# The context of keys and values in a linear-attention kernel: which operand stands, and who adds up the exponentials

## The reference

```python
qp = _softmax_kernel(q, proj[l], True)      # exp(scores - norm - row max) + 1e-4
kp = _softmax_kernel(k, proj[l], False)     # exp(scores - norm - max over all nodes) + 1e-4
k_sum = kp.sum(axis=2)
d_inv = 1.0 / einsum('bhnm,bhm->bhn', qp, k_sum)
ctx = einsum('bhnm,bhnd->bhmd', kp, v)
attn = einsum('bhnm,bhmd,bhn->bhnd', qp, ctx, d_inv)
```

## Time and profile before

| | |
|---|---|
| median of 3 runs | 1161.78 us (1157.0 to 1170.48) |
| profiled execution | 1162.99 us, span 1161.2 us |
| TensorE busy | 1088.6 us (94%) |
| VectorE, ScalarE, GpSimd busy | 697.2 (60%), 363.6 (31%), 148.2 us (13%) |
| context matmuls (line 706) | 512 records, 65.3 us |
| `at` matmuls (line 717) | 512 records, 61.6 us |
| attention stage of layer 0, layer 1 | about 119 to 230, 545 to 661 us of the span |

### The profile page before, as it was taken

One profiled execution on the slowest core, in us unless ns is written; L12 is line 12 of the kernel. 1 busy time (PEld: TensorE's weight loads), 2 busy tenths in 40 slices (PEclk: granted clock), 3 DMA queues, 4 the chain that ended last, 5 costly groups with the idle time before them and its releaser, 6 DMA issues.

```text
span 1161.2 us, 16045 instructions
## 1 busy us (share of the span) xinstructions
PE 1088.6 (94%) x5960; PEld 877.3 (76%) x5960; DVE 697.2 (60%) x1524; ACT 363.6 (31%) x667; POOL 148.2 (13%) x141
## 2 busy tenths in 40 slices
PE   3989799999999999998899999999999999999976
PEld 3767789888777777776898977777777888777632
DVE  7565677479676567457565479674753117723556
ACT  4234466525321311235466415221300012002222
POOL 4230202000000001200102000000000705000026
PEclk8998999999999999989899999999999999999999
DMA  6220101003311112000101003211247201100001
GB/s 211 97 100 1 38 2 38 1 5 91 91 47 63 56 46 78 0 1 1 38 1 38 1 5 115 71 61 50 96 156 252 73 1 37 35 1 1 1 18 55
DMA packets 34653, 60.15 MB, mean 52 GB/s; under 512 B 19440, under 2 KB 20400, under 8 KB 33936
## 3 DMA queue, kind: packets, MB, share of 16 engines
q1 hardware_dynamic: 12688, 41.21, 10.5%
q10 hardware_dynamic: 21888, 17.87, 4.8%
HBM read 48.59 MB, written 10.49 MB: 51 GB/s over the span
## 4 chain that ended last, share of the span: by engine, by line
PE 79%; DVE 10%; ACT 5%; issue 4%; POOL 1%; DMA 0%; ACTq 0%; POOLq 0%; DVEq 0%
PE ps_a L515 10%; PE ps_a L516 10%; PE ps_a L517 10%; PE ps_v L515 9%; PE ps_v L517 8%; PE ps_v L516 8%; PE ps_a L866 5%; PE ps_v L706 5%; PE ps_v L829 2%; PE ps_v L717 2%; PE ps_a L536 2%; PE ps_a L641 2%; DVE expk L1502 2%; ACT work L1037 2%; ACT expk L998 1%
## 5 line engine op out<-in xcount | busy, mean ns | idle before, releaser
L515 PE MATMUL ps_a<-ht_hi,w_hi 128*128 128x512 f32 x488 | 194.6, 399 | 2.7 <-DVE w_lo L1768 0.9
L516 PE MATMUL ps_a<-ht_lo,w_hi 128*128 128x512 f32 x488 | 191.9, 393 | 0.0
L517 PE MATMUL ps_a<-ht_hi,w_lo 128*128 128x512 f32 x488 | 191.6, 393 | 0.0
L948 ACT ACTIVATE work<-ps_a,col_sb 128x512 f32<-128x512 f32 x96 | 66.6, 719 | 203.0 <-PE ps_a L517 144.8
L515 PEld LDWEIGHTS ps_a<-ht_hi,w_hi 128*128 128x128 f32 x488 | 92.7, 190 | 26.1 <-DVE headmask_r L1467 1.3
L517 PEld LDWEIGHTS ps_a<-ht_hi,w_lo 128*128 128x128 f32 x488 | 92.7, 190 | 20.1
L516 PEld LDWEIGHTS ps_a<-ht_lo,w_hi 128*128 128x128 f32 x488 | 92.8, 190 | 19.3
L1621 DVE TENSOR_TENSOR xm<-ps_v,xm 128x512 f32<-128x512 f32 x80 | 55.2, 690 | 86.1 <-PE ps_v L517 85.7
L515 PE MATMUL ps_v<-w_hi,f_hi 128*128 128x512 f32 x256 | 101.7, 397 | 0.0
L517 PE MATMUL ps_v<-w_hi,f_lo 128*128 128x512 f32 x256 | 99.7, 389 | 0.0
L516 PE MATMUL ps_v<-w_lo,f_hi 128*128 128x512 f32 x256 | 99.6, 389 | 0.0
(11 more groups left out here) (228 smaller groups left out, 1941.3 us busy)
## 6 DMA issues: line engine op xcount, KB each, us to landing
stage<-wstream SPq DMA_DIRECT2D x62, 512.0 KB, 3.6
adj_d<-adj_win ACTq DMA_DIRECT2D x16, 256.0 KB, 2.9
adj<-adj_d ACTq DMA_DIRECT2D x2, 2048.0 KB, 12.1
xt_d<-xt_hi SPq DMA_DIRECT2D x2, 1024.0 KB, 5.0
xt_d<-xt_lo SPq DMA_DIRECT2D x1, 2048.0 KB, 11.4
ht_hi<-xt_d ACTq DMA_DIRECT2D x1, 2048.0 KB, 7.9
ht_lo<-xt_d ACTq DMA_DIRECT2D x1, 2048.0 KB, 12.8
x_again<-x ACTq DMA_DIRECT2D x8, 256.0 KB, 9.0
```

The source lines that it names most:

```text
L515: nc.tensor.matmul(ps, left[0], right[0], start=first, stop=False)
L516: nc.tensor.matmul(ps, left[0], right[1], start=False, stop=False)
L517: return nc.tensor.matmul(ps, left[1], right[0], start=False, stop=last)
L948: nc.scalar.activation(work[:, n % 4, :], psA[:, i % BANKS, :], func, **how).then_inc(a_empty, 1)
```

## The change

The operands of the context change places. The values of one head (64 columns) are now the stationary operand, and the exponentials of its node tile stream, all 256 features at once. The two heads of a pair stand on the left and right 64 columns of the array and write the upper and lower 64 partitions of one bank. The result is the context turned round, so VectorE copies it to `ctx_t`, and a new job, `turn_ctx`, turns it back with two transposes; VectorE copies that to `ctx_sb`. The columns of ones are gone from the products. In their place GpSimd adds up the 8 exponential tiles of each head with three adds (`k_part`, `k_sum`), and `turn_ctx` sums `k_sum` over the partitions by four matmuls with one column of ones. `ctx` moves to the end of step 1; `turn_ctx` stands where `ctx` stood. On GpSimd weight 3's split moves from pair 0 to pair 1, behind the adds.

```diff
@@ attention_order, ring_v_attention
         if s == 2 and g < STEPS:
-            yield "ctx", pair
+            yield "turn_ctx", pair
         if 1 <= g <= STEPS:
             yield "tr", g - 1
         if g >= 2:
             yield "at", g - 2
+        if s == 1 and g < STEPS:
+            yield "ctx", pair
...
-        elif what in ("ctx", "at"):
+        elif what in ("ctx", "turn_ctx"):
+            yield what, g
+        elif what == "at":
             yield from ((what, g, j) for j in range(2))
@@ tiles
-        ctx_sb = at("ctx_sb", [P, 2, 2, MT, DH + 1], f32, "ctx")
+        ctx_sb = at("ctx_sb", [P, 2, MT, 2, DH + 1], f32, "ctx")
+        ctx_t = at("ctx_t", [P, M], f32, "ht", 16 * KB)
+        k_part = at("k_part", [P, NT // 2, M], f32, "ht", 18 * KB)
+        k_sum = at("k_sum", [P, 2, M], f32, "ht", 22 * KB)
@@ TensorE
+                    elif what == "ctx":
+                        ps = bank("v", ("ctx", g))
+                        pe.wait_ge(expk_done, L * NH * NT + (2 * g + 2) * NT)
+                        if g == 0:
+                            pe.wait_ge(vsum_added, L * (NT - 1) + NT)
+                        for t in range(NT):
+                            for j in range(2):
+                                head = slice(DH * j, DH * (j + 1))
+                                nc.tensor.matmul(ps[head, 0:M], V[:, t, g, 1 + DH * j:1 + DH * (j + 1)],
+                                                 expk[g % 2][:, j, t, :], start=t == 0, stop=False)
+                        nc.tensor.matmul(ps[:, 0:M], vsum[:, g, 1:1 + P], eps_k[:].to_broadcast([P, M]), start=False,
+                                         stop=True).then_inc(v_full, 1)
+                    elif what == "turn_ctx":
+                        ps = bank("v", ("turn_ctx", g))
+                        written_v(("ctx", g))
+                        for m in range(MT):
+                            nc.tensor.transpose(ps[:, nodes(m)], ctx_t[:, nodes(m)], ident[:])
+                        pe.wait_ge(k_summed, L * NH + 2 * g + 2)
+                        for m in range(MT):
+                            for j in range(2):
+                                last = nc.tensor.matmul(ps[:, M + 2 * m + j:M + 2 * m + j + 1], k_sum[:, j, nodes(m)],
+                                                        V[:, 0, 0, 0:1], start=True, stop=True)
+                        last.then_inc(v_full, 1)
...
-                                    written_v(("ctx", pair, j))
+                                written_v(("turn_ctx", pair))
@@ GpSimd
                     nc.gpsimd.partition_all_reduce(kall[:, pair, :], kmax1[:, pair, :], P, RMAX).then_inc(kall_ready, 1)
                     if pair == 0:
+                        pool.wait_ge(a_full, a0 + (MIX_A[QK_ORDER[-1]] + 1))
+                    for j in range(2):
+                        done_ = 2 * (L * NH + 2 * pair + j)
+                        pool.wait_ge(expk_done, (L * NH + 2 * pair + j + 1) * NT)
+                        nc.gpsimd.tensor_tensor(k_part[:], expk[pair % 2][:, j, 0:NT // 2, :], expk[pair % 2][:, j, NT // 2:, :],
+                                                ALU.add).then_inc(k_parts, 1)
+                        pool.wait_ge(k_parts, done_ + 1)
+                        nc.gpsimd.tensor_tensor(k_part[:, 0:2, :], k_part[:, 0:2, :], k_part[:, 2:4, :],
+                                                ALU.add).then_inc(k_parts, 1)
+                        pool.wait_ge(k_parts, done_ + 2)
+                        nc.gpsimd.tensor_tensor(k_sum[:, j, :], k_part[:, 0, :], k_part[:, 1, :], ALU.add).then_inc(k_summed, 1)
+                        pool.wait_ge(k_summed, L * NH + 2 * pair + j + 1)
+                    if pair == 1:
                         load(3, ("a", QK_ORDER[-1]))
@@ VectorE
+                    if what == "ctx":
+                        nc.vector.tensor_copy(ctx_t[:], job("ctx", g)[:, 0:M]).then_inc(v_empty, 1)
+                        continue
+                    if what == "turn_ctx":
+                        ps = job("turn_ctx", g)
+                        nc.vector.tensor_copy(ctx_sb[:, g % 2, :, :, 0:DH], ps[:, 0:M].rearrange("p (m j d) -> p m j d", m=MT, j=2))
+                        nc.vector.tensor_scalar(ctx_sb[:, g % 2, :, :, DH], ps[:, M:M + 2 * MT].rearrange("p (m j) -> p m j", m=MT),
+                                                float(N * EPS_K), None, ALU.add).then_inc(v_empty, 1)
+                        continue
```

More of the change, by code:

```diff
@@ L697, in mix_layer @@
                             ps = bank("v", (what, g, j))
[L698 to L702, removed]
+                            if s == 0:
+                                written_v(("turn_ctx", pair))
+                            written_a(("tr", g, j))
+                            for n in range(2):
@@ L703, in mix_layer @@
                                 for m in range(MT):
[L704 to L709, removed]
@@ L710, in mix_layer @@
-                                last.then_inc(v_full, 1)
-                            else:
-                                if s == 0:
-                                    written_v(("ctx", pair, j))
[L714 to L721, removed]
+                                    last = nc.tensor.matmul(ps[:, n * (DH + 1):(n + 1) * (DH + 1)],
+                                                            work[:, 2 + j, nodes(2 * m + n)],
+                                                            ctx_sb[:, pair % 2, m, j, :],
+                                                            start=m == 0, stop=m == MT - 1)
@@ L1587, in mix_layer @@
                         (blocks, keys, bounds)[g]()
-                    for j in range(2):
[L1589 to L1593, removed]
+                    if what == "ctx":
[7 more added lines that the diff above has]
+                        continue
+                    for j in range(2):
+                        if what == "ddq":
                             i = MIX_A[("ddq", g, j)]
@@ L1603, in mix_layer @@
                             ps = job("at", g, j)[:, 0:2 * (DH + 1)].rearrange("p (t d) -> p t d", t=2)
-                            nc.vector.reciprocal(rden[:, g % 2, j, :], ps[:, :, DH * j]).then_inc(rden_done, 1)
+                            nc.vector.reciprocal(rden[:, g % 2, j, :], ps[:, :, DH]).then_inc(rden_done, 1)
                             dve.wait_ge(rden_done, L * 2 * STEPS + (2 * g + j + 1))
-                            nc.vector.tensor_tensor(V[:, 2 * s:2 * s + 2, pair, 1 + DH * j:1 + DH * (j + 1)], ps[:, :, 1 - j:1 - j + DH],
+                            nc.vector.tensor_tensor(V[:, 2 * s:2 * s + 2, pair, 1 + DH * j:1 + DH * (j + 1)], ps[:, :, 0:DH],
                                                     rden[:, g % 2, j, :].unsqueeze(2).to_broadcast([P, 2, DH]),
```

1 line of the change is left out of this document (added).

## The result

| | before | after |
|---|---|---|
| median (lowest to highest), 4 runs each | 1160.92 us (1157.0 to 1170.48) | 1200.24 us (1199.19 to 1202.91) |
| ratio to before, 95% interval | | 1.0321 [1.0282, 1.036] |
| span of the profiled execution, mean granted clock | 1161.2 us, 0.983 | 1197.4 us, 0.956 |
| GpSimd busy | 148.2 us | 218.9 us |

A forecast was written before the change was run, and what follows sets the result against it. TensorE sets the pace before; after the change GpSimd's chain to `at` was thought to decide. Delays of `at` 7.8, blocking 9 and clock 11 make 28; 1163 + 28 = 1191 us, range 1169 to 1212.

The forecast's parts named there:

- blocking (9 / 8): VectorE's work held up by GpSimd's long adds in the attention: 1.5 us once per pair, less about 3, +9 us.
- the clock (1.8): TensorE at 1.2 GHz after waiting for `at`: 1.8 us for each of six waits, +11 us, 0 if the clock holds.
- C: Context matmuls on TensorE: the two column halves run side by side, 4.0 us a pair, against 7.5 one after the other.
- rival 1: Faster: GpSimd's pause doesn't hold `k_bias`, so VectorE's road to `at` counts; 18 us less over both layers, say 1150; chance 0.09.
- the four roads to `at`: VectorE's road to each pair's first `at`: 8.0 against 9.9 us in three pairs, -1.9, and -3.4 in the fourth.
- The pause, and weight 3: GpSimd's 6.87 us pause before `kall` and weight 3's 7.0 us behind pair 1's sums delay its `at`: +7.6, layer 0 +8.8.
- the terms of +7.8: Shifts of each pair's first `at`, summed before blocking and clock: layer 0 5.7 us, layer 1 2.1 us.
- the forecast's 7.0, 1.14 and 8.5: Pair 1, layer 0, on the way from sums to `at`: weight 3's split 7.0, `block_all` 1.14, pause through copies and hand-over 8.5 us.
- 158.3: Time in us when pair 1's sums end on GpSimd: exponentials end at 153.71, second head's adds and hand-overs take 4.5.
- The pauses behind `kall`: Sign to look for on GpSimd: with those ahead of `kall`, pauses of about 7 us eight times a layer.

## Why the prediction was right, and where its sizes were off

The direction and the mechanism hold: GpSimd's pause delays `at` by way of VectorE's list. But it does not decide alone, as the forecast had it: the length of the adds costs nearly as much. The time came out 9 us above the forecast, inside its range. By pairs, the first `at` of layer 1 before (pair 0 in the earlier trace rows, 568.11) and after, TensorE's timelines:

```profile
596.67 1.90 PE L717 MATMUL ps_v<-ctx_sb,work 128*128 128x65 f32 x16
...
623.95 1.90 PE L717 MATMUL ps_v<-ctx_sb,work 128*128 128x65 f32 x16
...
649.71 1.90 PE L717 MATMUL ps_v<-ctx_sb,work 128*128 128x65 f32 x16
```
```profile
584.38 3.65 PE L734 MATMUL ps_v<-ctx_sb,work 128*128 128x65 f32 x16 [1.56 <-DVE ctx_sb L1624]
...
624.24 3.65 PE L734 MATMUL ps_v<-ctx_sb,work 128*128 128x65 f32 x16 [7.94 <-DVE ctx_sb L1624]
...
658.97 1.97 PE L734 MATMUL ps_v<-ctx_sb,work 128*128 128x65 f32 x16 [0.61 <-DVE ctx_sb L1624]
...
685.18 1.97 PE L734 MATMUL ps_v<-ctx_sb,work 128*128 128x65 f32 x16 [0.30 <-DVE ctx_sb L1624]
```

What each pair adds to the delay, against the prediction's terms with a share of blocking (9 / 8) in every pair and of the clock (1.8) in pairs 0 to 2. In layer 0, pair 2's `at` stood at 193.50 before; layer 1's pair 0 is counted from pair 3 of layer 0:

| us | layer 0: pair 0, 1, 2, 3 | layer 1: pair 0, 1, 2, 3 |
|---|---|---|
| predicted | +2.6, +11.7, +3.5, -2.3 | +0.2, +10.5, +3.5, -2.3 |
| measured | +1.4, +13.5, +4.6, -0.9 | -2.3, +11.3, +7.4, +0.5 |

- **The context (C)** was right: 4.3 us, predicted 4.0. The Trainium skill, "TensorEngine Tiling (Array Packing)", section "Theoretical Speedup", gives up to 2x for columns of 64; the trace agrees, since 16 products on column halves took 3.6 us (131.36 to 134.97), 0.23 each, against an estimate of 0.44 each one after the other.
- **What the context would give alone** was over-sized: 18 us in rival 1, and 8 (0.9929) to 12 (0.9892) in the runs without long adds, of which the second also has the biases behind the copies. The step that failed counted the four roads to `at` and left out that pair 0's was held by `kall` already, and probably (read from the trace, not shown by a run) that moving the context ahead of step 2's query scores leaves ScalarE idle and then late.
- **The pause, and weight 3** were right. Against rival 1's -18 the terms of +7.8 are a loss of 26; undoing weight 3's place took 0.9% (10 us) and the order on VectorE another 1.5% (18), together 28. Pair 1 is the worst in both layers, as forecast, by 13.5 and 11.3 us in place of 8 to 11. In layer 0 its chain ran as sized: from the end of the sums (163.76 + 0.73) to `at` it took 16.6 us, and the forecast's 7.0, 1.14 and 8.5 make 16.6. It began 6.2 us later than forecast (164.5, not 158.3; the forecast's own terms give 158.2, a rounding that changes nothing). The pauses behind `kall`, which the forecast also wanted to see, are hidden, because the adds wait longer for the exponentials (11.55 us at 150.67). That the lower clock behind these waits is part of the 28 can't be separated.
- **Blocking** was the mis-sized term: +9, measured 22 (1.0082 to 0.9892) and about 25 (1.0321 to 1.0101, with sums that end earlier); both are what the length of the adds does in all, by way of the clock too. I took 1.5 us once a pair. Other places that the trace shows are the biases in both heads, the key score copies queued behind them, and `sq_hi` and `sq_lo` of the stage ahead under pair 0's adds (TensorE waited 3.98 us there once a layer, 1.83 before and 1.98 with the adds shrunk).
- **The clock** was charged with 1.8 us for the one product behind each wait. After a wait it stayed at 0.50 for longer (12 us in the run without the adds): the mean over the span fell from 0.983 to 0.956. How much of that is on the path stays open.

So the three errors (context +6 to +10, blocking +13 to +16, clock at most -11) partly cancel: that 1191 was near is in part luck, for of its terms only the context's matmuls and the pause were well sized. The measured chain, from the change downwards: weight 3 back 10, biases behind the copies 18, adds short 22 us. What is then left, 12 us below the kernel before, belongs to the new context and the new order on VectorE together, which also frees pair 0 of a wait that the kernel before had.

## What to carry to other kernels

An engine that looks empty can be dear when its new work alternates with another kind: count its changes of kind and follow what is queued behind whoever waits for it. If such a wait must stay, let the waiting instruction stand behind what others need; here that order was worth nearly as much as removing the wait. A saving on the busiest engine counts only as far as the engine that feeds it next has its work earlier too.

## What the runs showed of the hardware

- GpSimd's change between TENSOR_TENSOR and all-reduce cost 5.8 to 7.5 us each time that it can be read, not only the first (6.65 and 5.97 in the change, 7.07 and 6.75 in the earlier trace rows); CAST behind TENSOR_TENSOR followed after 0.20.
- VectorE's SCALAR_TENSOR_TENSOR on two values per partition took up to 2.28 us under a 128x1024 add on GpSimd (0.16 without), and a CAST of 128x136 2.39 (0.23 without); TENSOR_REDUCE from PSUM kept its 0.68. The Trainium skill, "SBUF — State Buffer", section "Who interferes with whom", says that a VectorE instruction with two SBUF inputs contends with a GpSimd instruction that reads SBUF, that casts can contend, and that TENSOR_REDUCE never does; the trace agrees in all three.
- Behind TensorE's waits of 1.56 us (140.22) and 3.74 us (181.10) the granted clock was 0.55 and 0.50; behind one of 1.11 us (212.96) `at` took its full-speed 1.97.
- In the runs with the adds on VectorE, it adds 128x2048 in 2.28 us, about the time that GpSimd takes for 128x1024 (2.36).
